# First expert product computed transposed, step scales from a table, second norm's rows transposed by DMA, late slabs on VectorE

## The reference, cut to what matters

```
x1 = x + tanh(g_xattn) * moe(layernorm(x), token_ids, ctx)
x2 = x1 + tanh(g_ffn) * ffn(layernorm(x1), gate_w, up_w, down_w, scales)

moe: expert e of a token is min(id // 6250, 3); with M = ctx[e] (512 x 512) for all three weights:
     y = (silu(n @ M.T) * (n @ M.T)) @ M.T
ffn: gate = silu(n @ q(gate_w) * gate_scale); up = n @ q(up_w) * up_scale
     y = (gate * up) @ q(down_w) * down_scale; q rounds the weights to fp8 (e4m3)
```

## Time and profile before

| what | us |
|---|---|
| three executions | 422.85, 424.04, 427.60 (median 424.04) |
| the profiled execution | 427.73 |
| its span | 426.0 |
| TensorE busy | 395.8 (93%), 2,010 matmuls |
| VectorE busy | 234.5 (55%) |
| ScalarE busy | 183.2 (43%) |
| GpSimd busy | 168.9 (40%) |

### The profile page before, as it was taken

The page is one execution under the profiler, slowest core; times in us unless marked ns, Lnnn a source line. Parts: engine busy times, 40 slices in busy tenths (PEclk is TensorE's granted clock), DMA queues, the critical chain, the costliest instruction groups (busy, mean ns, idle before and its releaser), DMA issues.

```text
span 426.0 us, 6383 instructions
## 1 busy us (share of the span) xinstructions
PE 395.8 (93%) x2010; PEld 197.9 (46%) x2010; DVE 234.5 (55%) x503; ACT 183.2 (43%) x298; POOL 168.9 (40%) x190
## 2 busy tenths in 40 slices
PE   3959799999999999899999999999999999999991
PEld 2625445555555555444444444444444444444440
DVE  5676778988988678477642422224322225222244
ACT  4484547677786654865352222222222222222220
POOL 2437167764586658799630800001700002600003
PEclk9997989999999999999999999999999999999996
DMA  7575212211113101222000100000200000200002
GB/s 277 160 257 151 72 27 76 74 32 46 49 52 75 49 28 51 74 79 93 2 2 2 74 26 0 0 2 0 98 0 0 0 0 0 100 0 0 2 1 98
DMA packets 10508, 22.66 MB, mean 53 GB/s; under 512 B 1624, under 2 KB 1648, under 8 KB 10480
## 3 DMA queue, kind: packets, MB, share of 16 engines
q1 hardware_dynamic: 7920, 13.92, 10.5%
q0 software_dynamic: 2560, 8.39, 6.0%
HBM read 18.11 MB, written 4.19 MB: 52 GB/s over the span
## 4 chain that ended last, share of the span: by engine, by line
PE 84%; DVE 6%; POOL 4%; issue 2%; DMA 1%; ACT 1%; DVEq 0%; POOLq 0%; ACTq 0%
PE bank L1281 35%; PE bank L1194 24%; PE bank L1289 17%; PE bank L1126 5%; POOL w_sum L470 2%; POOL W L473 2%; PE bank L1148 1%; DVE Ml L794 1%; PE bank L1180 1%; DMA xs<-in_x,order 1%; DVE row_hot L777 1%; DVE w_big L836 1%; DVE xs L1107 1%; DMA ws<-in_L_ffn_down_w 1%; DVE X L1104 1%
## 5 line engine op out<-in xcount | busy, mean ns | idle before, releaser
L1281 PE MATMUL bank<-X,W 128*128 128x512 f16 (+1 forms) x768 | 173.5, 379 | 1.0 <-DVE late_norms L1046 1.0
L1281 PEld LDWEIGHTS bank<-X,W 128*128 128x128 bf16 x768 | 74.9, 98 | 92.0 <-DVE late_norms L1046 2.5
L1057 DVE SCALAR_TENSOR_TENSOR cs<-bank,up_mul,cs 128x512 f32<-128x512 f32 x48 | 36.0, 749 | 107.7 <-PE bank L1281 106.2
L1289 PE MATMUL bank<-W,cs 128*128 128x512 bf16 x376 | 88.7, 379 | 1.6 <-DVE X L856 1.6
L645 ACT ACTIVATE cs<-bank,gate_mul 128x512 f32<-128x512 f32 x48 | 32.9, 685 | 76.6 <-PE bank L1281 76.6
L506 POOL TENSOR_TENSOR xs<-xs,X 128x512 f32<-128x512 f32 x12 | 15.3, 1272 | 121.3 <-DVE X L1104 121.0
L652 ACT ACTIVATE cs<-cs 128x512 f16<-128x512 f32 x47 | 29.5, 628 | 76.0 <-DVE cs L1057 76.0
L1194 PE MATMUL bank<-Mh,X 128*128 x152 | 51.4, 401 | 8.6 <-DVE Ml L794 6.1
L1289 PEld LDWEIGHTS bank<-W,cs 128*128 128x128 f16 x376 | 36.5, 98 | 45.2 <-issue 1.8
L1065 DVE TENSOR_TENSOR cs<-cs 128x512 f16<-128x512 f32 x47 | 35.3, 751 | 37.1 <-ACT cs L652 36.0
L470 POOL TENSOR_TENSOR w_sum<-ws,w_big 128x512 f32<-128x512 f32 x36 | 47.3, 1313 | 5.1 <-DVE w_big L836 2.7
(11 more groups left out here) (145 smaller groups left out, 413.8 us busy)
## 6 DMA issues: line engine op xcount, KB each, us to landing
ws<-in_L_ffn_gate_w SPq DMA_DIRECT2D x12, 256.0 KB, 2.8
ws<-in_L_ffn_up_w SPq DMA_DIRECT2D x12, 256.0 KB, 2.6
ws<-in_L_ffn_down_w SPq DMA_DIRECT2D x12, 256.0 KB, 2.5
cs<-in_ctx SPq DMA_DIRECT2D x2, 1024.0 KB, 6.5
X<-in_ctx SPq DMA_DIRECT2D x2, 1024.0 KB, 7.0
xs<-in_x,order POOLq DMA_INDIRECT x16, 3.6
dsc<-in_L_ffn_down_scale SPq DMA_DIRECT2D x1, 256.0 KB, 7.3
out<-xs,order POOLq DMA_INDIRECT x16, 2.8
```

The lines of the kernel that those rows point to most:

```text
L1057: v.scalar_tensor_tensor(out=fuse[:, c % 2, :], in0=UP[c % 2][:], scalar=up_mul[:, c:c + 1], in1=sg[:, c % 2, :], op0=ALU.mult, op1=ALU.mu ...
L1281: ins = t_.matmul(dst[c % 2][:].rearrange("p (t i) -> p t i", t=TPG), w, x2_group(g, part, k), start=(k == 0 and part == 0), stop=(k == KC ...
L1289: ins = t_.matmul(ACC[t][:], fuse_part(g, c, part)[:, t * P:(t + 1) * P], W8[:, down_slab(c), :], start=(c == 0 and part == 0), stop=(c == ...
```

## The change

The first product is computed transposed: blocks of 128 x 128 of M are the stationary operand, the 128 tokens of the tile stream by, and Z holds 128 inner numbers by 4 x 128 tokens. h is then what the second product takes, without transposes: `hTh` and `hTl` are made of `h` in SBUF. From step 4 on the three scales of a step (`z_step`, `h_step`, `y_step`) come from tables that `step_tables` makes in step 3, at fixed addresses. The factor X_SCALE moves from the copies into the norm's statistics. The second norm writes its rows as a float16 high part (ScalarE) and low part (`x2_low`, now on GpSimd), and one transposing DMA per tile, issued by SP among the slab loads, puts them into `X2`; ScalarE's and VectorE's copies out of PSUM and TensorE's transposes for it are gone. Slabs 22 to 35 are rounded by VectorE alone, with two instructions each in place of one on VectorE and two on GpSimd.

```diff
+    TURNS = {26: 13, 30: 14, 32: 15}
+    BY_REGISTER = 4
-        Mh = sb("Mh", [P, E * KC * 512], F16)
+        Mh = sb("Mh", [P, E, KC, 512], F16)
...
+        x2n = sb("x2n", [P, 2, D], F32)
+        x2rows = sb("x2rows", [P, 2, 2 * D], F16)
...
-            for n in range(SLABS):
+            def turn_x2(tile):
+
+                sp.wait_ge(x2lo_done, tile + 1)
+                sp.dma_start_transpose(X2[:, tile].rearrange("p a k i -> p (a k) i"),
+                                       x2rows[:, tile % 2, :]).then_inc(x2T_in[tile % 2], 16)
+
+            for n in range(4):
                 load_slab(n)
+            loaded = 4
+            for s in range(STEPS):
+                if s >= X2_LAG:
+                    turn_x2(s - X2_LAG)
+                for n in slabs_of(s, s):
+                    load_slab(loaded)
+                    loaded += 1
+            for n in range(loaded, SLABS):
+                load_slab(n)
+                if n in TURNS:
+                    turn_x2(TURNS[n])
 
...
+            def x2_low(tile):
+
+                pool.wait_ge(x2n_done, tile + 1)
+                g.tensor_tensor(x2_row(tile, 1), x2n[:, tile % 2, :], x2_row(tile, 0),
+                                ALU.subtract).then_inc(x2lo_done, 1)
+
             def step(s, lo):
+                if lo >= X2_LAG:
+                    x2_low(s - X2_LAG)
                 ln_scalars(s + STATS1_LEAD, lo % 2, 0 if lo + STATS1_LEAD < TILES else 1,
                            2 if lo >= STATS2_LAG else 1)
...
-            for n in range(EARLY - 1, SLABS):
-                if n == EARLY + 1:
-                    ln_scalars(STEPS + STATS1_LEAD + 1, 0, 1, 2)
-                if n == LAST_DOWN + 2:
-                    ffn_norm(1, 2 * KC, IC)
-                round_slab(n, slab_slot(n))
+            round_slab(EARLY - 1, slab_slot(EARLY - 1))
+            x2_low(TILES - 3)
+            ln_scalars(STEPS + STATS1_LEAD + 1, 0, 1, 2)
+            x2_low(TILES - 2)
+            x2_low(TILES - 1)
+            ffn_norm(1, 2 * KC, IC)
...
             def normalise2(tile):
 
                 act.wait_ge(ln_done, tile + STATS2_LAG + STATS1_LEAD + 1)
-                if not (isinstance(tile, int) and tile == 0):
-                    act.wait_ge(x2T_done, tile)
+                if tile >= 2:
+                    act.wait_ge(x2T_in[tile % 2], 16 * (tile // 2))
                 r = tile + STATS1_LEAD + STATS2_LAG
-                a.activation(x2n[:], xs_tile(tile), ACT.Identity, scale=ln_col(r, 1, 0),
-                             bias=ln_col(r, 1, 1)).then_inc(x2n_done, 1)
-
-            def x2_high(tile, src):
-                act.wait_ge(x2T_done, tile + 1)
-                a.activation(x2_part(tile, 0), src[:].rearrange("p (k i) -> p k i", k=KC),
-                             ACT.Copy, scale=X_SCALE).then_inc(x2hi_done, 1)
+                mul, add = ln_col(r, 1, 0), ln_col(r, 1, 1)
+                a.activation(x2_row(tile, 0), xs_tile(tile), ACT.Identity, scale=mul, bias=add)
+                a.activation(x2n[:, tile % 2, :], xs_tile(tile), ACT.Identity, scale=mul,
+                             bias=add).then_inc(x2n_done, 1)
...
-                    a.activation(hTh[:], HT[:], ACT.Copy).then_inc(hhi_done, 1)
+                    a.activation(hTh[:], h[:], ACT.Copy).then_inc(hhi_done, 1)
...
                 act.wait_ge(z_done, s + 1)
-                if lo >= 1:
-                    act.wait_ge(h_done, s)
-                a.activation(silu_z[:], Z[:], ACT.Silu, scale=z_scale[:, ds(e, 1)]).then_inc(silu_done, 1)
+                if lo >= BY_REGISTER:
+                    act.wait_ge(tables_done, 1)
+                    scale = z_step[:, s:s + 1]
+                else:
+                    scale = z_scale[:, ds(expert_of(words, s), 1)]
+                a.activation(silu_z[:], Z[:], ACT.Silu, scale=scale).then_inc(silu_done, 1)
...
-                if lo >= X2_LAG:
-                    x2_high(s - X2_LAG, X2T)
...
-            x2_high(TILES - 3, XT)
...
-            normalise2(TILES - 2)
...
-            x2_high(TILES - 2, XT)
-            normalise2(TILES - 1)
...
-            x2_high(TILES - 1, XT)
...
                     if first:
                         late_second(c)
+                        if c < 4:
+                            normalise2(TILES - 4 + c)
...
-                v.tensor_tensor(hTl[:], HT[:], hTh[:], ALU.subtract).then_inc(hlo_done, 1)
+                v.tensor_tensor(hTl[:], h[:], hTh[:], ALU.subtract).then_inc(hlo_done, 1)
-                x_low(x2_part(tile, 1), XT[:].rearrange("p (k i) -> p k i", k=KC), x2_part(tile, 0),
-                      xhi_done, tile + 1).then_inc(xlo_done, 1)
+                dve.wait_ge(xhi_done, tile + 1)
+                v.tensor_tensor(x2_part(tile, 1), XT[:].rearrange("p (k i) -> p k i", k=KC), x2_part(tile, 0),
+                                ALU.subtract).then_inc(xlo_done, 1)
 
...
 
-                dve.wait_ge(y_step_done, s + 1)
+                if s < BY_REGISTER:
+                    dve.wait_ge(y_step_done, s + 1)
+                else:
+                    dve.wait_ge(tables_done, 1)
...
+            def step_tables():
+
+                later = slice(BY_REGISTER, STEPS)
+                n = STEPS - BY_REGISTER
+                v.tensor_tensor(step_hot[:, :, later], e_of[:, later].unsqueeze(1).to_broadcast([P, E, n]),
+                                iota_q[:, 0:E].unsqueeze(2).to_broadcast([P, E, n]),
+                                ALU.is_equal).then_inc(step_hot_done, 1)
+                dve.wait_ge(ys_done, E)
+                dve.wait_ge(step_hot_done, 1)
+                for i, scales in enumerate((z_scale, h_scale, y_scale)):
+                    ins = v.tensor_tensor(step_sel[:, i, :, later], step_hot[:, :, later],
+                                          scales[:].unsqueeze(2).to_broadcast([P, E, n]), ALU.mult)
+                ins.then_inc(step_sel_done, 1)
+                dve.wait_ge(step_sel_done, 1)
+                v.tensor_reduce(y_all[:, later], step_sel[:, 2, :, later].rearrange("p e s -> p s e"), AX.X,
+                                ALU.add).then_inc(y_all_done, 1)
+                v.tensor_reduce(z_step[:, later], step_sel[:, 0, :, later].rearrange("p e s -> p s e"), AX.X, ALU.add)
+                v.tensor_reduce(h_step[:, later], step_sel[:, 1, :, later].rearrange("p e s -> p s e"), AX.X, ALU.add)
+                dve.wait_ge(mask_done, 1)
+                dve.wait_ge(y_all_done, 1)
+                v.tensor_tensor(y_step[:, later], mask[:, later], y_all[:, later], ALU.mult).then_inc(tables_done, 1)
...
+                if lo >= BY_REGISTER:
+                    dve.wait_ge(tables_done, 1)
                 if lo >= 1:
-                    dve.wait_ge(hT_done, s)
-                v.scalar_tensor_tensor(out=h[:], in0=Z[:], scalar=h_scale[:, ds(e, 1)], in1=silu_z[:],
+                    dve.wait_ge(hlo_done, s)
+                scale = h_step[:, s:s + 1] if lo >= BY_REGISTER else h_scale[:, ds(e, 1)]
+                v.scalar_tensor_tensor(out=h[:], in0=Z[:], scalar=scale, in1=silu_z[:],
                                        op0=ALU.mult, op1=ALU.mult).then_inc(h_done, 1)
 
...
-                step_y_scale(s, e)
+                if lo < BY_REGISTER:
+                    step_y_scale(s, e)
...
-                if lo >= X2_LAG:
-                    x2_low(s - X2_LAG, X2T).then_inc(x2lo_done, 1)
...
+                if lo == BY_REGISTER - 1:
+                    step_tables()
...
                 for n in range(EARLY + 2 * c, min(EARLY + 2 * c + 2, SLABS)):
-                    slab_big(n, slab_slot(n))
+                    slot = slab_slot(n)
+                    dve.wait_ge(abs_done, n + 1)
+                    dve.wait_ge(q_done, n)
+                    v.scalar_tensor_tensor(out=w_sum[:], in0=w_big[:, slot], scalar=FP8_FLOOR, in1=ws[:, slot],
+                                           op0=ALU.max, op1=ALU.add).then_inc(sum_done, 1)
+                    dve.wait_ge(sum_done, n + 1)
+                    v.scalar_tensor_tensor(out=W8[:, n, :], in0=w_big[:, slot], scalar=FP8_FLOOR, in1=w_sum[:],
+                                           op0=ALU.max, op1=ALU.subtract, reverse1=True).then_inc(q_done, 1)
 
...
-            x2_low(TILES - 2, XT).then_inc(x2lo_done, 1)
-            x2_low(TILES - 1, XT).then_inc(acc_free, TPG)
...
 
-            def product(dst, e, high, low, done):
-
-                n = 0
-                for k in range(KC):
-                    mh = Mh[:, ds(e * (KC * 512) + k * 512, 512)]
-                    ml = Ml[:, ds(e * (KC * 512) + k * 512, 512)]
-                    for lhs, rhs in ((high(k), mh), (high(k), ml), (low(k), mh)):
-                        ins = t_.matmul(dst[:], lhs, rhs, start=(n == 0), stop=(n == 3 * KC - 1))
-                        n += 1
-                ins.then_inc(done, 1)
-
-            def turn_h(s):
-                pe.wait_ge(h_done, s + 1)
-                transpose4(HT, h, hT_done)
-
```

(49 more changed lines are left out.)

61 lines of the change are left out of this document (30 added, 31 removed).

## The result

The changed kernel takes 450.15 us (median of four executions, 449.03 to 451.25), the kernel before 425.09 (four, 422.85 to 427.60): a ratio of 1.059, interval 1.052 to 1.066, slower. Forecast were 445.9 us and 418 to 462. The profiled execution took 449.0 us, span 447.3; the sum had 449.6 for it.

A forecast was written before the change was run, and what follows sets the result against it. The prediction took packed TensorE work, 6.63 us a middle step, to bound the kernel before; terms summing to +21.9 us made 427.73 into 449.6, less 3.7 for the median gave 445.9 us, range 418 to 462.

The forecast's parts named there:

- the sum: All terms of the change added, +21.9 us on the profiled 427.73 us, giving 449.6 us for the profiled execution.
- Dispatch: First product: register work for addresses makes its 48 matmuls take 4.7 us, against 2.6 for the array.
- The rival with load and matmul in turn: First product: 128-column loads not hidden, 0.08 us a pair, 3.8 us per product; 430 us, chance 0.08.
- The loop: Steps 4 to 14: 3.15 us through silu, h, x1_low and addresses plus 4.7 make 7.85 us a step, +12.7 us.
- TensorE waiting behind x1_low: Sign of being right, in the middle steps: TensorE waits behind x1_low, with its clock still full.
- fit exactly: Middle steps: transposes of x, second product and norms, 3.1 us, fit into the 3.15 us between first products.
- The loop of 6.4 us: Kernel before, middle steps: 2.59 + 2.97 + 0.04 + 0.77 us, just under 6.63 of packed TensorE work.
- the rival of no change: First product: about 3.2 us as part of the dispatch is hidden, loop 6.35 us; 424 us, chance 0.08.
- Early products: Before step 4: products 0 and 2 each grow from 2.6 to 4.7 us, +4.2; product 1 nothing, product 3 +0.5.
- Tables: Step 3: 8 small VectorE instructions and four waits, 2.2 us ahead of h_low, +1.0 us on the path of h(4).
- this rival: Second norm: the transposing DMA in SP's queue paces the steps, from about 5.2 us each; 482 us, chance 0.07.
- Feed-forward part: Its start: fewer transposes and less waiting, but VectorE rounds slabs; net -1.2 us, between -3 and +2.

The follow-up runs named there:

- static_expert: Changed kernel with the first product always naming expert 0's matrices at fixed addresses; 429.0 us, ratio 1.011.
- ahead_spread: Changed kernel with all 40 first-product addresses worked out between the matmuls of the preceding second product (ahead of the waits for the first two); 427.9 us, ratio 1.009.
- first run: The changed kernel as first measured and traced, against the kernel before; 450.15 us, ratio 1.059.
- ahead_five: Changed kernel with the expert's and tile's number worked out ahead of the waits for h and x1_low; 441.4 us, ratio 1.042.
- old_product: Changed kernel with the 512-column first product, TensorE's transposes of h and their waits back; 423.2 us, ratio 0.9985.
- second run: The changed kernel, unchanged, measured again beside the last experiments; 445.9 us, ratio 1.051.
- old_no_tables: As old_product, with the scales of every step by register, without step_tables; 419.8 us, ratio 0.989.
- only_transposed: Kernel before with only the transposed first product, h from SBUF and four-dimensional Mh and Ml; 452.9 us, ratio 1.067.
- dma_norm_only: As old_no_tables, with the late slabs rounded by GpSimd again; 423.2 us, ratio 0.996.

## Why the prediction was right

1. **Dispatch.** Forecast 36 register instructions and 4.7 us for a product; there are 36, and 4.33 to 4.7 us up to step 15. A group of three with two register instructions was put at 0.12 + 0.12 + 0.025 and took 0.24 to 0.28; the first four groups, with three, take 0.39 to 0.49. static_expert and ahead_spread take the instructions away and leave 3.0 and 2.62 us. The rival with load and matmul in turn is out: 0.055 us a pair in ahead_spread, where the Trainium skill (TensorE: Matmul & The Clock Gate, back-to-back issue gap) gives about 81 ns; here the measurement decides, and the 128 x 128 load (95 to 98 ns each) is hidden behind the matmuls.
2. **The loop.** Forecast 3.15 us from last matmul to next product, measured 3.19; a step of 7.85, measured 7.71 to 7.73 on average (84.8 / 11): the 11.1 to 11.3 against 12.7 us are this 0.12 to 0.14 a step, and it lies in the product (4.46 us on average in the first run, not 4.7). The 3.15 us were read as a wait behind x1_low, and "TensorE waiting behind x1_low" was to be a sign of being right. That sign did not come as idle time: TensorE is busy 7.52 of 7.52 us, as its queue, which the prediction put at 3.1 us and found to "fit exactly", ends with the chain. ahead_five shows what follows: with the chain 0.5 us shorter the 3.19 us stay. Steps 15 to 17 came to 7.03 on average and not 7.45. Step 15 takes 7.44; in steps 16 and 17 the product takes 3.9 us from first to last start and not the 4.7 forecast.
3. **The floor under the old form.** The loop of 6.4 us that I read into the kernel before was too long for a step that has 6.19 of TensorE work: old_product runs at 6.19. The sum counts the last matmul twice: 12 x 0.216 = 2.59 reaches to its end, the 2.97 us start at its start (104.35). From first to last start a product takes 2.37 us, and 2.37 + 2.97 + 0.04 + 0.77 = 6.15 is just under 6.19. The number that was wrong was not used in the sum, only in old_product's expectation and in the rival of no change.
4. **Early products.** Forecast +4.7 without the tables, measured +4.4 in the second run and +8.7 in the first. In the first, product 2 starts 16.0 us behind product 1 (13.0 before, 12.4 in the second run), and its table of waits lists what no other trace has:

```profile
ACT Mh L575 <- remote: 3.7, 1, 3.7
```

   Products 0 to 1 grew by 2.2 (2.1 forecast), 2 to 3 by 2.6 and 3.1 (2.1), as product 2 ran at half clock (0.50) in the first run and in part in the second: 5.29 and 5.16 us from first to last start, against some 4.5 at full clock. Product 0 ran at half clock in part as well (0.67 over 21.13 to 26.30). Step 3 grew by 0.25 to 0.4 (0.5 forecast), against a step of before in which product 3 had run at half clock itself (4.04 us in place of 2.38).
5. **Tables.** +1.0 was forecast, from 8 instructions and 2.2 us. In the changed kernel they run in step 4 and take 2.5 us (69.24 to 71.7); the next product starts 3.34 us behind the last matmul there (3.52 in the second run) in place of 3.19, so the term was 0.15 to 0.33 and not 1.0. In a packed kernel they cost 2.6 us in step 4 and 3.3 between the medians (old_product to old_no_tables), since VectorE holds them 4.2 us and not 2.2: two instructions are held by GpSimd, which y_step's row had shown. The chain is 0.49 us a step shorter with them, where 0.2 us had been counted; what that is worth in the step is not shown (only_transposed).
6. **Second norm and DMA.** Landing was put between 2.5 and 7 us and hidden. The page of the changed kernel, part 6, against the earlier trace rows:

```profile
ws<-in_L_ffn_down_w SPq DMA_DIRECT2D x12, 256.0 KB, 3.2
...
X<-x2rows SPq DMA_TRANSPOSE x16, 3.1
```

   3.1 us for eight 128 x 128 blocks, so this rival is out for the changed kernel, and so is the estimate of 10.5 us from the Trainium skill's figure for one block (VectorE: DVE Perf Modes, the three transpose paths): the blocks do not run one by one. Its mechanism, the DMA's place in SP's queue, is real all the same: in dma_norm_only, where x2_low comes late, the slab load behind it costs 4.7 us. h_low, from two SBUF operands, has 682 ns in the median and 1,761 at worst in the changed kernel and is hidden in 7.7 us steps, as forecast; in ahead_spread's 6.2 us steps its median is 990.
7. **Feed-forward part.** Forecast -1.2, measured +0.5. The fourth gate product starts 18.4 us in (17.8 forecast, 19.0 before); 1.1 us are lost behind it. The fifth and sixth unit take 5.59 and 7.65 us (5.18 and 5.99 before), the next two are 0.9 shorter together. At the end of the sixth TensorE waits for the weights' norms on VectorE:

```profile
218.06 3.63 PE L1336 MATMUL bank<-X,W 128*128 128x512 f16 x16 [1.34 <-DVE late_norms L1108]
```

   The forecast had VectorE level with TensorE in these units (5.2 and 5.17 us) and no term for this wait.
8. **From the profile to the median.** The sum was 449.6, too high by 4.4 against the second run's 445.2 (1.8 of it the start to product 0, which the change does not touch) and level with the first only by its stall. The 3.7 us taken off, as the profiled execution of before lay above its median, made 445.9. The traces show what that execution had: product 0 starts at 20.7 to 21.2 us in nine of the thirteen traces and at 22.6 to 23.2 in four, before among them, and exactly in these four the ten matmuls ahead of it (line 1180 before, 1239 after) take 3.6 to 3.9 us in place of 2.32. In these four the matmuls start 0.427 us apart up to some 19.5 us, the pace of half clock, and 0.216 apart behind it; in the nine others they are 0.216 apart from the first. So in the four the clock rose later. Besides, product 3 of before ran at half clock (4.04 us, 2.38 in the other four traces with the 512-column form); that product 1 did so too (4.67 us) is no peculiarity, as three of those four have it. The forecast's 445.9 lies on the second run's median by two errors that cancel, the high sum and a correction that was not reasoned from any stretch. That is luck; the mechanism and the sizes of its main terms are not.
